# A decoder layer's scan on one core: the masked C times B is kept in an accumulator bank, and x is transposed into the bank of its own projection

## The reference

```python
proj = hidden_states @ W_in.T                 # z, xBC and dt
xBC = silu(conv1d(xBC))                       # 4 taps
dt = softplus(dt + dt_bias)
x_dt = x * dt
L = exp(segsum(dt * A))                       # lower triangular, per head
y = (C B^T * L) x_dt + D * x                  # 64 heads of 64, one B and C for all heads
out = rmsnorm(y * silu(z)) * norm_w @ W_out.T
```

## Time and profile before

| | |
|---|---|
| median of 3 runs | 1648.02 us (1647.4 to 1648.2) |
| the profiled execution | 1647.34 us, of which its span is 1645.6 us |
| busy in the span: PE / DVE / ACT / POOL | 97% / 75% / 73% / 50% |
| first iteration's transposes to the last scan | 41.9 to 913 us of the span |

### The profile page before, as it was taken

How to read it: one execution, slowest core, us unless ns; L and a number is a source line. 1 busy time by engine, 2 the same in 40 slices (tenths; PEclk the granted TensorE clock), 3 DMA queues, 4 the chain that set the end, 5 groups by cost and what they waited for, 6 DMA issues and landing times. The chain is left out here.

```text
span 1645.6 us, 29169 instructions
## 1 busy us (share of the span) xinstructions
PE 1593.7 (97%) x9876; PEld 1279.0 (78%) x9876; DVE 1235.2 (75%) x1955; ACT 1204.3 (73%) x2512; POOL 824.6 (50%) x674
## 2 busy tenths in 40 slices
PE   4999999999999999999999999999979999999999
PEld 3677777777777777777777667877758989999888
DVE  6899999999898999889888756667676533344355
ACT  5999999999999999999999566666634234344331
POOL 5688895555565555555555312211124563335460
PEclk8999999999999999999999999999989999999999
DMA  7555555444544454565552100000134333222231
GB/s 279 187 171 193 187 182 167 154 154 154 165 156 147 152 166 154 169 233 172 163 169 92 57 1 14 14 14 27 62 125 163 128 122 100 91 91 94 81 101 50
DMA packets 76239, 209.85 MB, mean 128 GB/s; under 512 B 9152, under 2 KB 32960, under 8 KB 74304
## 3 DMA queue, kind: packets, MB, share of 16 engines
q1 hardware_dynamic: 70432, 181.90, 33.0%
q0 software_dynamic: 5664, 26.09, 4.6%
HBM read 170.99 MB, written 36.96 MB: 126 GB/s over the span
## 5 line engine op out<-in xcount | busy, mean ns | idle before, releaser
L1027 PE MATMUL banks<-pair_hi,m_wxz 128*128 128x512 f32 x1024 | 351.4, 404 | 4.3 <-DVE pair_lo L675 2.3
L393 POOL TENSOR_TENSOR m_mat<-m_mat,m_cb_off 128x512 f32<-128x512 f32 x128 | 166.4, 1300 | 305.9 <-DVE m_mat L762 300.4
L752 DVE SCALAR_TENSOR_TENSOR m_xc<-banks,m_cw,m_xc 128x510 f32<-128x510 f32 (+2 forms) x384 | 284.9, 742 | 12.5 <-ACT m_xc L506 7.7
L520 ACT ACTIVATE m_mat<-m_a_all,m_cum 128x256 f32<-128x256 f32 x512 | 259.3, 506 | 0.0
L1084 PE MATMUL m_ps_out<-m_won,m_gT 128*128 128x256 f32 x1024 | 252.4, 389 | 0.0
L1027 PEld LDWEIGHTS banks<-pair_hi,m_wxz 128*128 128x128 f32 x1024 | 194.0, 189 | 44.5 <-DVE m_zs L774 4.6
L1084 PEld LDWEIGHTS m_ps_out<-m_won,m_gT 128*128 128x128 f32 x1024 | 184.9, 190 | 38.1 <-issue 17.2
L523 ACT ACTIVATE m_mat<-m_a_all,m_cum 128x128 f32<-128x128 f32 x512 | 204.1, 399 | 0.0
L1027 PE MATMUL banks<-pair_lo,m_wxz 128*128 128x512 f32 x512 | 201.3, 393 | 0.0
L1068 PE MATMUL m_ps_y<-m_mat,m_xdt 128*64 128x256 f32 (+1 forms) x2048 | 194.7, 332 | 0.4 <-DVE m_xdt L780 0.4
L1068 PEld LDWEIGHTS m_ps_y<-m_mat,m_xdt 128*64 128x64 f32 x2048 | 126.8, 136 | 82.9 <-issue 39.9
(11 more groups left out here) (352 smaller groups left out, 3446.2 us busy)
## 6 DMA issues: line engine op xcount, KB each, us to landing
m_a_all<-a_by_head SPq DMA_DIRECT2D x128, 512.0 KB, 4.1
m_wxz<-w_split SPq DMA_DIRECT2D x96, 512.0 KB, 4.8
w_split<-m_wxz SPq DMA_DIRECT2D x32, 512.0 KB, 2.9
raw<-in_w_gate_up POOLq DMA_DIRECT2D x9, 1280.0 KB, 6.6
raw<-in_w_xz SPq DMA_DIRECT2D x32, 256.0 KB, 3.9
raw<-in_w_down POOLq DMA_DIRECT2D x9, 640.0 KB, 7.7
x_sorted<-f_gT_hi SPq DMA_DIRECT2D x1, 4992.0 KB, 16.7
f_xg<-x_sorted SPq DMA_DIRECT2D x39, 128.0 KB, 2.6
```

The lines of the kernel that those rows point to most:

```text
L393: pool.tensor_tensor(off, off, cb_off[:, g * BG:(g + 1) * BG, :].rearrange("p b t -> p (b t)").unsqueeze(1) .broadcast_to([P, HPT, BG * P] ...
L520: act.activation(first_rows(u, h, b), a_all[u][:, h, b * SEQ:(b + 1) * SEQ].rearrange("p (j t) -> p j t", t=P), ACT.Relu, bias=cum[:, t, h ...
L752: dve.scalar_tensor_tensor(out=out[:, :, k:], in0=ps[:, :, 0:SEQ - k], scalar=cw[:, c, TAPS - 1 - k:TAPS - k], in1=out[:, :, k:], op0=ALU. ...
L1027: last = pe.matmul(ps[:, :], w, a, start=m == 0, stop=m == len(terms) - 1)
```

## The change

Three things change places, and PSUM still has eight banks in use.

1. The bank that was `ps_t` becomes `ps_cb`. It holds the masked C times B of the group that is at work, 2 x 256 columns. `matrices` reads it from there, and no longer from SBUF.
2. The next group's masked C times B is still made early, into `cb_next` in SBUF, and copied into the bank by a new DVE instruction (`cb_move`), once per group for the last three groups, just ahead of the first `matrices` of the group. For the first group, `masked` writes into the bank at once.
3. x is transposed into `ps_x[n % 2]`, the bank of its own projection, which silu_x(n) has read for the last time; `x_times_dt` reads it from there. So x_proj(n + 2) now waits for x_times_dt(n) (`xdt_done`) where it waited for silu_x(n). transposes(n) no longer waits for x_times_dt(n - 1).

```diff
-        cb_diag = sb("cb_diag", [P, 2 * BG, 2 * P])
+        cb_next = sb("cb_next", [P, BG, 2 * P])
...
-        ps_x, ps_z, ps_t = shared[0:2], shared[2], shared[3]
+        ps_x, ps_z, ps_cb = shared[0:2], shared[2], shared[3]
...
+        def cb_now(b):
+            return ps_cb[:, b * 2 * P:(b + 1) * 2 * P]
...
             def masked(h, b):
                 ...
-                dve.tensor_tensor(cb_diag[:, h % 2 * BG + b, :], ps_s[:, 0:2 * P], mask[:], ALU.mult).then_inc(cb_done, 1)
+                out = cb_now(b) if h == 0 else cb_next[:, b, :]
+                dve.tensor_tensor(out, ps_s[:, 0:2 * P], mask[:], ALU.mult).then_inc(cb_done, 1)
+
+            def cb_move(g):
+                dve.wait_ge(cb_done, (g + 1) * BG)
+                dve.tensor_copy(ps_cb[:, :], cb_next[:].rearrange("p b t -> p (b t)")).then_inc(cb_moved, 1)
...
             def matrices(n):
-                g, diag = n // NCT % 2, diagonal(n % 3)
+                diag = diagonal(n % 3)
                 dve.wait_ge(exp_done, n + 1)
-                if n % NCT == 0:
-                    dve.wait_ge(cb_done, (n // NCT + 1) * BG)
-                dve.tensor_tensor(diag, diag, cb_diag[:, g * BG:(g + 1) * BG, :].rearrange("p b t -> p (b t)").unsqueeze(1)
-                                  .broadcast_to([P, HPT, BG * 2 * P]), ALU.mult).then_inc(mat_done, 1)
+                if n == 0:
+                    dve.wait_ge(cb_done, BG)
+                elif n % NCT == 0:
+                    dve.wait_ge(cb_moved, n // NCT)
+                dve.tensor_tensor(diag, diag, ps_cb[:, :].unsqueeze(1).broadcast_to([P, HPT, BG * 2 * P]), ALU.mult)\
+                    .then_inc(mat_done, 1)
...
             def x_times_dt(n):
-                                  ps_t[:, :].rearrange("p (t h d) -> p t h d", t=TPG, h=HPT),
+                                  ps_x[n % 2][:, :].rearrange("p (t h d) -> p t h d", t=TPG, h=HPT),
...
                 elif more:
+                    if (n + 1) % NCT == 0:
+                        cb_move((n + 1) // NCT)
                     matrices(n + 1)
...
             def x_proj(n):
                 if n >= 2:
-                    pe.wait_ge(x_silu, n - 1)
+                    pe.wait_ge(xdt_done, n - 1)
...
             def transposes(n):
                 pe.wait_ge(x_silu, n + 1)
-                if n >= 1:
-                    pe.wait_ge(xdt_done, n)
-                else:
-                    pe.wait_ge(xT_lo_done, EARLY)
                 for q in range(TPG):
-                    last = pe.transpose(ps_t[:, q * P:(q + 1) * P], xs[:, n % 2, q * P:(q + 1) * P], ident)
+                    last = pe.transpose(ps_x[n % 2][:, q * P:(q + 1) * P], xs[:, n % 2, q * P:(q + 1) * P], ident)
...
             def context_keys(p):
                 if p < 2:
-                    pe.wait_ge(x_silu, N - 1 + p)
+                    pe.wait_ge(xdt_done, N - 1 + p)
                 ...
                 else:
-                    pe.wait_ge(xdt_done, N)
+                    pe.wait_ge(mat_done, N)
```

More of the change, by code:

```diff
@@ L186, in mamba_phase @@
             sem(n) for n in ("halved", "bc_ready", "bc_scaled", "bc_copied", "bc_conv", "bc_tanh", "bc_done"))
-        cb_ready, cb_done = sem("cb_ready"), sem("cb_done")
+        cb_ready, cb_done, cb_moved = sem("cb_ready"), sem("cb_done"), sem("cb_moved")
         (x_ready, z_ready, t_ready, y_ready, out_ready, sum_ready) = (
@@ L204, in tile_bank @@
                 return ps_s[:, n % 2 * HID:(n % 2 + 1) * HID]
-            return (ps_out[:, 0:HID], ps_out[:, TG:TG + HID], ps_t[:, 0:HID], ps_x[1][:, 0:HID])[n % 4]
+            return (ps_out[:, 0:HID], ps_out[:, TG:TG + HID], ps_cb[:, 0:HID], ps_x[1][:, 0:HID])[n % 4]
         def tile_whole(n):
```

## The result

The changed kernel takes 1651.66 us in the median, the kernel before 1647.48 beside it on the same chips: a ratio of 1.0025, 95% interval 1.0019 to 1.003. It is slower by about 4 us, as forecast (1652.5, sum of terms +4.8). One of the changed kernel's 22 executions, a slow one of 2642.33 us, is left out of the ratio. The profiled execution took 1651.37, with a span of 1649.6 against 1645.6.

The account below looks back on a forecast made before the run. DVE was taken to pace 110 to 198 us, PE 700 to 900. Up to iteration 20 the terms left PE at -0.1; 0.69 and 4.2 made +4.8 on 1647.34, 1652.1, put at 1652.5 us; range 1648 to 1657.

Parts of the forecast that it names:

- Iteration 2: Early in the first group: x_times_dt is late, so the x projection waits and the scan comes 1.63 us later.
- The turns: Second and third iterations of groups two to four: DVE is late behind mean_out; 1.40 us three times, 4.2 in all.
- Iteration 49: At 391 us, x_times_dt is late and the scan comes 0.69 us later, at 392.95 against 392.26.
- PE-paced iterations: Where PE paces, the z projection covers the new wait with 0.24 us to spare: cost 0.
- the margin rival: The 0.24 us margin in PE-paced iterations isn't there; 0.10 in each of 85 iterations adds 8.5: 1661 us, chance 0.08.
- The start 0.14 and the scan 1.69 behind x_times_dt: Where DVE is late, the x projection starts 0.14 us and the scan 1.69 us after x_times_dt ends.
- The copy: cb_move, three of 128 x 512, at most 0.69 us each, hidden in DVE's idle time: 0; uncovered 2.1 in all.
- The accumulator operand itself: matrices reading one operand from PSUM takes 1.21 us, as from SBUF without a collision; no added fixed time.
- the stretch from 8 to 20: DVE-paced part of the first group: shorter matrices return 3.57 us, 0.5 lost, 1.35 wait at iteration 20; PE at -0.1.
- the 0.5 put as lost: In the DVE-paced stretch, 0.5 us of the 3.57 gain is lost where x_times_dt must wait for the transposes.
- the rival of the freed stretch: From 110 us DVE's other two-SBUF-operand instructions are freed too and PE paces: +1.4 us, 1649.1, chance 0.3.
- each is paid once: At the four late places the delay is paid once, not per iteration: a later PE finds DVE caught up.

Follow-up runs that it names:

- wait_only: The changed kernel's transposes into x's bank and wait at the x projection, on the kernel before, masked C times B staying in SBUF; 1653.78 us, 1.0036 of before.
- cast_late: The kernel before, with POOL's cast of the next weights moved behind its own product of the matrices; 1650.71 us, 1.0024 of before.
- cast_small: The kernel before, with POOL's cast cut to 64 elements per partition, leaving out seven eighths of it; 1644.04 us, 0.9975 of before.
- mean_late_3: The changed kernel, mean_out behind the first two taps at the turns, x_times_dt ahead of them in iterations 2-8, 34, 48, 49, 66, 98; 1647.38 us, 1.0001 of before.
- xdt_first: The changed kernel, with x_times_dt moved from behind the two conv taps to right behind the gate in every iteration; 1649.92 us, 1.0018 of before.

## Why the prediction was right

The time, the sign and the mechanism came out as put, and most terms by their size. The lag gives them one by one:

- *Iteration 2*: +1.63 foretold, +1.65.
- *The turns*: 4.2 foretold, 1.34 + 1.37 + 1.44 = 4.15. The three were priced from one, iteration 98; each is in fact spread over two iterations (33 and 34, 65 and 66, 97 and 98), both held.
- *Iteration 49*: 0.69 foretold, 0.66, of which 0.22 falls to 45 to 48.
- *PE-paced iterations*: 0 foretold, 0. The lag stands still from 101 to 125, and the margin rival is refuted.
- *The start 0.14 and the scan 1.69 behind x_times_dt*: 0.15 and 1.70.
- *The copy*: hidden. It takes 0.69, its upper bound, and no step of the lag stands where it runs.
- *The accumulator operand itself*: 1.207 to 1.211 in the median for 1.212 of SBUF without a collision. By the rows it was 0, and it is 0. The step there was luckier than it reads: with one row of each size (0.692 for 512 elements with such an operand, 1.212 for 1024 without) any split between a fixed part and a price per element fits, and only this trace settles it. The rule of the Trainium skill weighed in the prediction ("VectorE: DVE Perf Modes", the section on the TRN2 errata) would have made it an estimated 0.06 longer; this trace doesn't show that.

**The term that was mis-sized** is the stretch from 8 to 20: 1.63 - 3.57 + 0.5 + 1.35 put PE at -0.1 behind it, and it stood at -0.87. The wait at its end was right: the scan of 20 lagged 1.37 more than x_times_dt, for a foretold 1.35. What DVE catches up was put too small: x_times_dt of 20 stood at -2.23 (192.01 - 194.01, less the 0.23 of the start) for -1.44. I counted the relief of matrices alone, and 1.09 of its 3.57 belongs to the instruction of 2.297 at 100.8 us, which lies ahead of the stretch and which the subtraction held, not the cast. Summed between the transposes of 8 and 21, matrices fell from 18.25 to 15.71, the taps of the next group's B and C from 4.00 to 2.88, and their silu (two instructions) from 2.45 to 1.70: 2.5 that I had priced and 1.9 that I hadn't. In wait_only, which has the wait and not the operand, taps and silu stand at 3.53 and 2.37, so 1.3 of the 1.9 came with the operand. Of the 4.4 in all DVE kept 3.9; the 0.5 put as lost, an estimate without a row of its own, came out by luck. Behind it stands the rival of the freed stretch, which named those other instructions: half of its mechanism is there, but PE did not pace the stretch, and its 1649.1 did not come. The -0.77 by which the term was off is most of the 0.8 between the sum (+4.8) and the span (+4.0).

Why DVE and POOL hold each other, the prediction left at a reading of the earlier trace rows. wait_only, cast_late and cast_small show it: matrices with two SBUF operands is stretched beside a POOL instruction that began ahead of it (the cast from 9 to 14), not without one, and not with one operand in an accumulator bank. The Trainium skill states it in "SBUF — State Buffer", the section on who interferes with whom: a VectorE instruction with two SBUF inputs contends with a GpSimd instruction that reads SBUF, and one with at most one input there, outside the modes that use two ports, doesn't. By the section on SBUF's two separate sides, on the same page of the Trainium skill, whichever of the two starts first has the shared ports for the whole instruction, and the other is blocked. The traces agree: 1.223 at most in 128 with one SBUF input, 1.25 for a cast of 64 elements that had to wait out its neighbour, and an end 1.08 to 1.09 behind POOL's for every stretched matrices of the kernel before and of wait_only.

What was right for a reason that held only in part: "each is paid once". It is for a single late place, but mean_late_3 shows that taking a hold away by order can put it into the next iteration, and xdt_first that it can come back as a wait for silu_x.

## What to carry to other kernels

A bank that is shared by two steps in a row saves memory and adds a wait; price it at the places where the engine that frees the bank is late (the start, the turns between groups, the loaded stretch), from the lateness that the trace already shows there, and take it as covered elsewhere. If one engine's instruction is stretched by another's, look at all its neighbours with the same operand placement: here moving one operand out of the contended memory relieved them together, while reordering (cast_late) picked a new victim. And price the relief only where the relieved engine paces. And an instruction that waits, put ahead of others that are ready on an in-order engine, costs little until a later change takes away its cover.

## What the runs showed that I had not expected

A cast of 128 x 64 takes 0.23 us alone and 1.25 beside a VectorE instruction of 1.41: the hold has the length of the neighbour and not of the work. At the end of the phase the product that began 0.19 us behind VectorE's split, and not ahead of it, took 1.0 more; with what the early x_times_dt had put off there, the sums of the last group came 2.4 later. And 5.5 us of lead at the end of the phase (cast_small) became 3.6 in the time: in its profiled execution 2.3 of the lead is lost behind the phase, 1.4 of that between 1215 and 1230 us, where its granted clock falls once more (0.79 from 1222 to 1230).
